# Selective stage: a batch's row statistics taken one turn ahead, and x's second-norm update moved behind the spectral products

## The reference, cut to what matters

```python
xin = layernorm(x)                                    # before the block; x_text below
Q, K, V = xin @ Wq, ctx @ Wk, ctx @ Wv                # 4 heads of 32, 120 context rows
scores -> top 32 of 120 per row -> softmax -> mean over heads -> c_t = attn_mean @ V
u   = layernorm(xin, g_norm_in, b_norm_in) * (1 + gate * scale_in(c_t)) + gate * shift_in(c_t)
y   = s4d(u)                                          # long convolution, done as products with cosines and sines
xt  = xin + y * (1 + gate * scale_out(c_t)) + gate * shift_out(c_t)
xt  = xt + gelu(layernorm(xt) @ W1 + b1) @ W2 + b2
x   = x + layernorm(xt, g_norm_out, b_norm_out)
```

## Time and profile before

| what | value |
|---|---|
| median of 3 runs | 4438.66 us (4436.61 to 4439.12) |
| profiled execution, its own time | 4439.32 us |
| its span (first to last instruction) | 4436.7 us |
| busy shares of the span | PE 92%, PEld 72%, DVE 73%, ACT 51%, POOL 13% |
| selective stage in the span | about 3519 to 4209 us |

### The profile page before, as it was taken

One profiled execution on the slowest core, in us unless ns is written; L12 is line 12 of the kernel. 1 busy time (PEld: TensorE's weight loads), 2 busy tenths in 40 slices (PEclk: granted clock), 3 DMA queues, 4 the chain that ended last, 5 costly groups with the idle time before them and its releaser, 6 DMA issues. The chain is left out here.

```text
span 4436.7 us, 70562 instructions
## 1 busy us (share of the span) xinstructions
PE 4068.3 (92%) x23248; PEld 3212.8 (72%) x23248; DVE 3231.7 (73%) x7695; ACT 2273.5 (51%) x5395; POOL 575.3 (13%) x1096
## 2 busy tenths in 40 slices
PE   6997997999789999999999999999999679999788
PEld 5886775777567787787777777777787457667565
DVE  6995666766757777777777777777776588888457
ACT  3554664555346556555655556556564134444244
POOL 1331001010320000000000000000023323333111
PEclk9998998999889999999999999999999589999999
DMA  3001000000000000000000000000001100000011
GB/s 97 0 0 38 0 0 1 0 0 0 15 7 1 2 4 2 5 1 5 1 2 5 2 5 1 2 5 2 2 1 44 33 1 1 0 0 0 5 37 39
DMA packets 34246, 40.38 MB, mean 9 GB/s; under 512 B 6270, under 2 KB 30470, under 8 KB 33930
## 3 DMA queue, kind: packets, MB, share of 16 engines
q1 hardware_dynamic: 33196, 36.90, 2.8%
q10 hardware_dynamic: 800, 0.33, 0.0%
HBM read 32.76 MB, written 4.19 MB: 8 GB/s over the span
## 5 line engine op out<-in xcount | busy, mean ns | idle before, releaser
L1724 ACT ACTIVATE global_prob_t_high<-psum 128x512 fp32r<-128x512 f32 x960 | 569.7, 600 | 590.1 <-PE psum L1838 590.1
L1632 DVE TENSOR_TENSOR global_prob_t_low<-psum,global_prob_t_high 128x512 fp32r<-128x512 f32 x960 | 657.0, 690 | 250.5 <-ACT global_prob_t_high L1724 236.6
L1638 DVE TENSOR_REDUCE global_top<-psum 128x1 f32<-128x480 f32 x1024 | 666.7, 658 | 111.9 <-PE psum L1798 106.6
L1796 PE MATMUL psum<-global_prob_t_high,global_v_low 128*128 128x512 f32 x960 | 455.8, 475 | 0.8
L1796 PE MATMUL psum<-global_k_high,global_q_low 128*128 128x480 f32 x1024 | 391.1, 382 | 16.9 <-ACT spare L1745 14.5
L1798 PE MATMUL psum<-global_k_high,global_q_high 128*128 128x480 f32 x1024 | 391.7, 383 | 0.0
L1797 PE MATMUL psum<-global_k_low,global_q_high 128*128 128x480 f32 x1024 | 389.2, 380 | 0.0
L1797 PE MATMUL psum<-global_prob_t_low,global_v_high 128*128 128x512 f32 x960 | 379.6, 395 | 0.0
L1798 PE MATMUL psum<-global_prob_t_high,global_v_high 128*128 128x512 f32 x960 | 379.3, 395 | 0.0
L1745 ACT ACTIVATE spare<-psum,global_bias 128x480 f32<-128x480 f32 x512 | 337.1, 663 | 16.6 <-DVE global_bias L1641 15.1
L1745 ACT ACTIVATE global_prob<-psum,global_bias 128x480 f32<-128x480 f32 x512 | 337.0, 661 | 1.4
(11 more groups left out here) (470 smaller groups left out, 8471.0 us busy)
## 6 DMA issues: line engine op xcount, KB each, us to landing
x_res<-in_x SPq DMA_DIRECT2D x8, 512.0 KB, 9.9
moe_we<-in_expert_t SPq DMA_DIRECT2D x8, 512.0 KB, 7.6
out<-x_res SPq DMA_DIRECT2D x16, 256.0 KB, 2.1
cho_wqkv<-in_L_ffn_Wqkv SPq DMA_DIRECT2D x2, 1536.0 KB
self_ctx_t<-in_ctx_t SPq DMA_DIRECT2D x2, 1440.0 KB, 13.9
sel_w<-in_L_xattn_W SPq DMA_DIRECT2D x2, 1024.0 KB, 11.0
global_ctx_t<-in_ctx_t SPq DMA_DIRECT2D x1, 1440.0 KB
sel_ctx_t<-in_ctx_t SPq DMA_DIRECT2D x1, 1440.0 KB
```

The lines of the kernel that those rows point to most:

```text
L1632: dve.tensor_tensor(dst, psum, high.bitcast(F32), ALU.subtract).then_inc(ready.sem, 1)
L1638: ins = dve.tensor_reduce(top[:, c:c + 1], w.psum[:, c, 0:chunk], AX.X, ALU.max)
L1724: act.activation(dst, psum, ACT.Copy).then_inc(ready.sem, 1)
L1796: pe.matmul(to, lhs_low, rhs_high, start=start, stop=False)
```

## The change

- The pipeline gets a fifth role, `M`, one batch ahead of T. VectorE measures the rows of batch M (not T) at the same place in its turn, and GpSimd makes the scales of M. `rstd_of_normed` gets a second buffer for it. New waits keep the single buffers of statistics and scales safe.
- ScalarE writes xl of T as the first thing of its turn, ahead of the copies of k and v.
- VectorE's L2480 and L2483 (y times g_norm_out, added to x) move from before the spectral products to behind the first half of u, just ahead of L2512.
- `over_iterations` writes out five turns (now = -3 to 1), loops over ten (now = 2 to 11), and writes out five (now = 12 to 16); the T and F roles keep their place relative to `now`. The turn now = -3 holds only M = 0.
- No arithmetic on data is added or taken away, and no DMA is touched.

```diff
-    rstd_of_normed = sb("rstd_of_normed", [P, LANES])
+    rstd_of_normed = [sb(f"rstd_of_normed{n}", [P, LANES]) for n in range(2)]
...
     def over_iterations(eng, iteration):
-        for n in range(-2, 2):
...
-        with eng.Fori(1, B // 2 - 1) as t:
-            iteration((2 * t + 2, 0), (2 * t + 1, 1), (2 * t, 0), 2 * t - 1)
-            iteration((2 * t + 3, 1), (2 * t + 2, 0), (2 * t + 1, 1), 2 * t)
-        iteration(None, (B - 1, 1), (B - 2, 0), B - 3)
-        iteration(None, None, (B - 1, 1), B - 2)
-        iteration(None, None, None, B - 1)
+        for n in range(-3, 2):
+            iteration((n + 3, (n + 3) % 2), (n + 2, n % 2) if n >= -2 else None, (n + 1, (n + 1) % 2) if n >= -1 else None,
+                      (n, n % 2) if n >= 0 else None, n - 1 if n >= 1 else None)
+        with eng.Fori(1, B // 2 - 2) as t:
+            iteration((2 * t + 3, 1), (2 * t + 2, 0), (2 * t + 1, 1), (2 * t, 0), 2 * t - 1)
+            iteration((2 * t + 4, 0), (2 * t + 3, 1), (2 * t + 2, 0), (2 * t + 1, 1), 2 * t)
+        for n in range(B - 4, B + 1):
+            iteration((n + 3, (n + 3) % 2) if n + 3 < B else None, (n + 2, n % 2) if n + 2 < B else None,
+                      (n + 1, (n + 1) % 2) if n + 1 < B else None, (n, n % 2) if n < B else None, n - 1)
...
# GpSimd
-                if T:
-                    scale_rows(pool, chain, "a", T[0])
-                    scale_normed_rows(pool, chain)
+                if M:
+                    i, p = M
+                    need(pool, "xl_ready", i - 1)
+                    scale_rows(pool, chain, "a", i)
+                    need(pool, "u_base", i - 2)
+                    scale_normed_rows(pool, chain, p)
...
# VectorE
-                if T:
-                    stats("a", T[0], x_tile(T[0]))
-                if done is not None:
-                    need(dve, "yn_ready", done)
-                    link(dve.tensor_tensor(y, y, rows["g_norm_out"][:, :].unsqueeze(1).to_broadcast([P, LANES, D]),
-                                           ALU.mult))
-                    need(dve, "x_biased", done)
-                    dve.tensor_tensor(both_tiles(done), both_tiles(done), y, ALU.add).then_inc(sig("x_updated").sem, 1)
+                if M:
+                    i, p = M
+                    need(dve, "rstd_normed", i - 1)
+                    stats("a", i, x_tile(i))
                 if now:
...
                                       ALU.add).then_inc(sig("u_base").sem, 1)
+                if done is not None:
+                    need(dve, "yn_ready", done)
+                    link(dve.tensor_tensor(y, y, rows["g_norm_out"][:, :].unsqueeze(1).to_broadcast([P, LANES, D]),
+                                           ALU.mult))
+                    need(dve, "x_biased", done)
+                    dve.tensor_tensor(both_tiles(done), both_tiles(done), y, ALU.add).then_inc(sig("x_updated").sem, 1)
...
# ScalarE
                 if T:
                     i, p = T
+                    need(act, "rstd_a", i)
+                    need(act, "base_ready", i - 2)
+                    normalise("a", lambda s: w.x_res[:, i * LANES + s, :], xl[p]).then_inc(sig("xl_ready").sem, 1)
                     need(act, "kv_ready", i)
...
                 if T:
                     i, p = T
-                    need(act, "rstd_a", i)
-                    need(act, "base_ready", i - 2)
-                    normalise("a", lambda s: w.x_res[:, i * LANES + s, :], xl[p]).then_inc(sig("xl_ready").sem, 1)
                     need(act, "xl_t_psum", i)
```

More of the change, by code:

```diff
@@ L2319, in over_iterations @@
     def over_iterations(eng, iteration):
-        for n in range(-2, 2):
-            iteration((n + 2, n % 2), (n + 1, (n + 1) % 2) if n >= -1 else None, (n, n % 2) if n >= 0 else None,
-                      n - 1 if n >= 1 else None)
-        with eng.Fori(1, B // 2 - 1) as t:
-            iteration((2 * t + 2, 0), (2 * t + 1, 1), (2 * t, 0), 2 * t - 1)
-            iteration((2 * t + 3, 1), (2 * t + 2, 0), (2 * t + 1, 1), 2 * t)
-        iteration(None, (B - 1, 1), (B - 2, 0), B - 3)
-        iteration(None, None, (B - 1, 1), B - 2)
-        iteration(None, None, None, B - 1)
+        for n in range(-3, 2):
[7 more added lines that the diff above has]
+                      (n + 1, (n + 1) % 2) if n + 1 < B else None, (n, n % 2) if n < B else None, n - 1)
     def scale_rows(pool, chain, half, n):
@@ L2336, in scale_rows, with scale_normed_rows @@
         pool.tensor_tensor(offset[:, :], offset[:, :], r[:, :], ALU.mult).then_inc(sig(f"rstd_{half}").sem, 1)
-    def scale_normed_rows(pool, chain):
+    def scale_normed_rows(pool, chain, p):
         _, mean_var, r, _ = norms["a"]
-        r2 = rstd_of_normed[:, :]
+        r2 = rstd_of_normed[p][:, :]
         chain.link(pool.tensor_tensor(r2, mean_var[:, :, 1], r[:, :], ALU.mult))
@@ L2355, in _, with iteration @@
             chain.link(pool.memset(minus_one[:, :], -1.0))
-            def iteration(T, F, now, done):
+            def iteration(M, T, F, now, done):
                 chain.restart_always()
@@ L2502, in iteration @@
                     for s in range(LANES):
-                        ins = dve.scalar_tensor_tensor(u_in[p][:, s, :], xl[p][:, s, :], rstd_of_normed[:, s:s + 1],
+                        ins = dve.scalar_tensor_tensor(u_in[p][:, s, :], xl[p][:, s, :], rstd_of_normed[p][:, s:s + 1],
                                                        rows["g_norm_in"][:, :], ALU.mult, ALU.mult)
```

## The result

| | before | after |
|---|---|---|
| median, measured side by side | 4437.64 us (4435.28 to 4439.12, 4 runs) | 4394.48 us (4391.79 to 4395.2, 4 runs) |
| ratio, 95% interval | | 0.9902 [0.9885, 0.9919] |
| profiled execution, its span | 4439.32, 4436.7 us | 4394.44, 4392.3 us |
| selective stage, L2355's memset to the last L2473 (after: L2476) | 684.3 us | 645.2 us |

Lines shift: L2473 is now L2476, L2480 and L2483 are L2509 and L2512, L2488 to L2492 are L2487 to L2491, L2512 is L2517, L2521 is L2526, L2683 is L2688, L2706 is L2711, L2384 and L2450 are L2387 and L2453.

What follows compares the result with a forecast made beforehand. Two late norms, y on VectorE and xl on TensorE's side, were taken to bound each turn. 23.5 + 6.8 - 4.6 + 6.5 + 2.3 = 34.5 us off 4438.66 gave 4404.2 us, range 4397 to 4418.

Steps and rivals of the forecast that it cites:

- the thirteen first pieces: L2473 to L2512 in turns now = 1 to 13: shorter by 23.5 us in all, bounds 18.2 and 27.3.
- the last two turns: now = 14 and 15: TensorE waits less for L2492 without y in front; 6.5 us gained, bounds 4.7 and 7.9.
- T = 1: Second batch: statistics a turn old remove waits at L2503 and L2521; 6.8 us gained, bounds 5.5 and 7.1.
- T = 0: First batch: GpSimd copies the context after all its scales, delaying k and v; costs 4.6 us (4.2 to 5.5).
- The per-turn gain: L2512 comes earlier each turn: 1.9 us in ten loop turns, about 1.5 in three after an unrolled turn.
- the tie of two engines: At L2512 VectorE is ready at 3791.74 and TensorE at 3791.78; 1.9 us per loop turn taken for it.
- Rival B: VectorE becomes the bound of L2512, held up by GpSimd scale steps: 4409 or 4418 us; chance 0.27.
- part 4: Turns 12 and 13 leave the loop and become unrolled: 2.3 us gained, bounds 0 and 2.7.
- C: Something not hanging on L2512 holds L2473, so the steady gain is lost: 9.2 us gained, 4430; chance 0.10.
- D: GpSimd's scales of M delay h and the hidden layer: 9 us slower, 4448 us; chance 0.04.

Runs made afterwards that it cites:

- small_y_update: Kernel after with both of VectorE's steps of y cut from 256 columns to 8: 4392.06 us, ratio 0.9904.
- toss_lost: Kernel before with two empty GpSimd instructions ahead of L2336: 4446.19 us beside 4436.0, ratio 1.0020.
- no_loop: Kernel after with all turns written out and no hardware loop: 4388.54 us, ratio 0.9893.
- before_again: Kernel before, unchanged, measured and profiled a second time: 4433.12 us, ratio 0.9999.
- part 1: Kernel after with y's two steps put back ahead of the spectral products, measured twice: 4432.82 us (ratio 1.0000) and 4438.36 us.
- part 2 alone: Kernel before with only y's two steps moved behind the first half of u: 4420.82 us, ratio 0.9972.
- ctx0_early: Kernel after with GpSimd copying batch 0's context before its scales: 4391.29 us, ratio 0.9907.

## Why the prediction was wrong

The mechanism was right at each step; the sum was too small. Inside the stage it is 4.6 us short, most of it in two terms: the thirteen first pieces (23.5 forecast, 26.2 measured) and the last two turns (6.5 and 8.0). Outside the stage it counts nothing, and the code ahead of it took 5.1 us less in the profile of after. In-stage terms, each as forecast and as the profiles of before and after give it:

| term | forecast | measured |
|---|---|---|
| 13 first pieces (now = 1 to 13) | 23.5 | 26.2 |
| T = 1, first to second scores | 6.8 | 7.2 |
| T = 0, memset to first scores | -4.6 | -4.2 |
| now = 14 and 15 | 6.5 | 8.0 |
| turns 12 and 13 written out, second pieces | 2.3 | 2.3 |
| now = 0 (0.6 later), rest | 0 | -0.4 |
| stage | 34.5 | 39.1 |
| code ahead of the stage | not counted | 5.1 |
| code behind it | not counted | 0.2 |

- *The per-turn gain, "1.9 in ten loop turns for the tie of two engines" and "about 1.5" in three, was undersized.* A turn gained 2.1 us in the loop (12.51 to 10.39) and 1.6 to 1.8 in the three that follow an unrolled one (12.31 to 10.76, 12.47 to 10.71, 12.51 to 10.76): 26.2, within its bounds of 18.2 and 27.3. The tie cost nothing: L2491 was not held up, and small_y_update shows that VectorE's lateness isn't what sets L2517.
- *Rival B* did not happen. The Trainium skill ("SBUF — State Buffer", "Who interferes with whom") has the one issued first hold the other up. That agrees with L2344's 1.17 behind L2491, and with L2336's 0.71 in toss_lost, where it starts 0.03 behind L2480; at a start 0.01 apart the trace doesn't show who was first. In this kernel GpSimd, not VectorE, came second, so it was the one to pay, and its result has no reader in the turn.
- *The last two turns* gained 8.0, just above the upper bound of 7.9. The waits fell to 0.64 and 1.51 as announced, and both backward products went back to 3.72 from 5.41 and 5.31: the whole of the clock's 1.6 each, where I had taken about half. These two turns are not steady in before: their first pieces add up to 27.8, 28.6 and 27.2 in its three profiles (19.8 in each of after's), so the term is 7.4 to 8.8 by the profile chosen.
- *T = 0, T = 1 and part 4* came within 0.5 us. Turns now = 12 and 13 were 35.18 and 35.54 (35.6 forecast), loop pairs 72.6 (73.1). L2453 in the loop still takes 2.1 beside L2387, in written-out turns 1.16. The measured 2.3 of part 4 includes 0.36 in now = 11, since that turn became the last one of the loop. The cost of nothing for more written-out code holds: no_loop, with ten more turns, has 35.54 in each.
- *Rivals C and D*: no wait appeared at the turn's end, and none on GpSimd that anything followed. Both are excluded by the pair of 72.6. (C's price was added up wrongly: the low ends of its terms are 0, 4.7 and 0, so 4434 and not 4430.)
- *The failed step is the base of the sum:* "4438.66 - 34.5 = 4404.2" takes one profiled execution as if it differed from the next by the change alone, and code ahead of the stage by nothing. With the stage's 39.1 the time would have been 4438.66 - 39.1 = 4399.6, inside the range. The other 5.1 us is the stage's start, 3518.95 before and 3513.90 after, in identical code. It has gathered over the blocks ahead: VectorE's first L2047 stands at 3420.4 before and 3415.8 after. Over the profiles the start lies at 3519.0, 3515.4, 3514.6 for before, 3513.9, 3512.6, 3513.3 for after, and between 3511.5 and 3518.5 for the ten others. The seven profiles of kernels built on before average 3515.2, the nine built on after 3513.5, and the two groups overlap. So most of the 5.1 is a spread of executions; what makes it, and whether the code's place in memory has a part of up to 2 us, stays open.
- The base profile also had the shortest stage of the three of before: 684.3, then 695.2 and 686.0, 688.5 on average, against 645.2 to 645.3 in each of after's. That is 43 us, about the difference of the medians. How much of what is missing between the forecast and the medians is the start and how much is slow turns of before can't be told, since only one execution of each batch is traced.
- The kernel before also carries turns of 14.2 us in some executions (toss_lost, before_again). The two profiles compared here had none in now = 1 to 13, so they explain none of the 44 us between them; they can be in the medians of before, 4433.8 to 4440.8 over its batches. In the profiles the change takes them away too: L2480 no longer stands beside L2336, TensorE waits for at most 0.8 us between L2476 and L2517 of a full turn, and no full turn of after's three profiles fell.

## What to carry to other kernels

When two late results hold a turn on two engines, cost the removal of each alone before summing: here 0 and 13 us made 41 together. Compare stages from one fixed instruction of the trace, not spans, and take a second profile of the kernel before: identical code ahead of the stage moved by up to 7.4 us, as much as some terms of the sum. Look for instructions of VectorE and GpSimd that start within some hundredths of a us of each other ahead of a matmul chain, for there the time can differ from one execution to the next.

## What the runs showed of the hardware

- Which of two instructions that start within 0.04 us of each other is held up can cost 1.7 us: L2336 at 0.20 or 0.71 to 0.75, then TensorE's wait of 1.4 or 2.0, then in part of the turns a granted clock below 1.00 over the next products (0.79 over 5.8 us in toss_lost).
- The fall behind a wait isn't certain. Waits of 1.83 to 1.85 were followed by it in 3 and in 5 of the nine loop turns (now = 3 to 11) of the two profiles of part 1, waits of 2.0 in 5 of 7 (before_again) and 5 of 11 (toss_lost); in the loop turns of the other profiles of before and of part 2 alone, with waits of 1.43 to 1.51, by none. It can also come behind shorter waits elsewhere: in the turn now = 14 waits of 1.40 and 0.69 were followed by it in three of seven profiles (0.81 over L2750's 8.86 us in ctx0_early).
- TensorE work that nobody reads cost nothing that shows: 1.03 us of filler in a wait, ratio 0.9990 [0.9981, 0.9999]. With it the waits were at most 1.21, and no loop turn of its one profile fell, though L2336 lost five times.
- A turn in the hardware loop costs 0.8 us more than the same turn written out (36.3 against 35.54): L2453's 0.9 to 1.0 beside GpSimd's L2387 is more than all of it. And writing out 10 more of them cost nothing that the profile shows.
